# Windowed attention stage of a two-layer decoder: scores first in each unit, exponents ahead of the projections' copies, shift ahead of the weights' copy

## What is computed

```
q, k, v = x @ Wq.T, x @ Wk.T, x @ Wv.T        # 16 query heads, 4 key heads, head size 128
q, k = rms_norm(q), rms_norm(k)               # over the head, times (1 + w)
q = q * cos + rotate_half(q) * sin            # k likewise
scores = q . k / sqrt(128), masked to 0 <= distance <= 64
att = softmax(scores); ctx = att @ v
x = x + ctx @ Wo.T
```

## Time and profile before

| | us |
|---|---|
| median of three runs | 1591.7 (1590.38 to 1596.24) |
| the profiled execution, its own time | 1597.39 |
| its span, first to last instruction | 1595.6 |
| busy in the span: PE, DVE, ACT, POOL | 1339.1, 1099.5, 810.9, 629.7 |
| mean granted clock of PE | 0.929 of 2.4 GHz |
| the windowed stage, first normalised x to last output | about 729 to 1243 |

### The profile page before, as it was taken

One profiled execution on the slowest core, in us unless ns is written; L12 is line 12 of the kernel. 1 busy time (PEld: TensorE's weight loads), 2 busy tenths in 40 slices (PEclk: granted clock), 3 DMA queues, 4 the chain that ended last, 5 costly groups with the idle time before them and its releaser, 6 DMA issues. The chain is left out here.

```text
span 1595.6 us, 26439 instructions
## 1 busy us (share of the span) xinstructions
PE 1339.1 (84%) x7985; PEld 1027.9 (64%) x8032; DVE 1099.5 (69%) x2086; ACT 810.9 (51%) x1811; POOL 629.7 (39%) x693
## 2 busy tenths in 40 slices
PE   6775278888699999984898998998998788987998
PEld 3332155555588888873677776777776465656887
DVE  5999588889456767568777777777776466653443
ACT  2222078888454343435565665665665255652332
POOL 3220466556561000006666566656665333220000
PEclk9988589999799999996999999999999799998999
DMA  9000133331000000002000000000000000000000
GB/s 367 41 0 0 40 99 87 79 79 40 1 1 1 1 0 0 1 1 96 1 1 1 0 0 0 0 0 0 0 0 1 5 3 3 2 1 1 14 13 27
DMA packets 30303, 40.24 MB, mean 25 GB/s; under 512 B 4320, under 2 KB 25824, under 8 KB 28704
## 3 DMA queue, kind: packets, MB, share of 16 engines
q1 hardware_dynamic: 30240, 39.45, 7.9%
HBM read 28.96 MB, written 2.10 MB: 19 GB/s over the span
## 5 line engine op out<-in xcount | busy, mean ns | idle before, releaser
L1704 ACT ACTIVATE wi_weights<-wi_psum,wi_bias,wi_scale 128x128 f32<-128x128 f32 x256 | 113.9, 454 | 113.0 <-DVE wi_bias L1814 113.0
L1479 POOL TENSOR_TENSOR wi_straight<-wi_straight,wi_crossed 128x512 f32<-128x512 f32 x80 | 110.0, 1374 | 5.8 <-DVE wi_crossed L1800 5.7
L846 DVE TENSOR_REDUCE gq_top<-gq_psum 128x4 f32<-128x512 f32 x128 | 86.8, 678 | 32.0 <-PE gq_psum L733 31.2
L1467 POOL TENSOR_TENSOR wi_scratch<-wi_sums,wi_eps 128x4 f32<-128x4 f32 x80 | 35.9, 449 | 159.7 <-DVE wi_sums L1783 158.3
L1805 DVE TENSOR_REDUCE wi_top<-wi_psum 128x4 f32<-128x512 f32 x64 | 44.0, 688 | 74.7 <-PE wi_psum L1594 74.7
L800 ACT ACTIVATE gq_weights<-gq_weights 128x512 f32<-128x512 f32 x128 | 81.1, 634 | 25.2 <-DVE gq_weights L854 23.9
L1018 POOL TENSOR_TENSOR ex_scratch<-ex_squares,ex_eps 128x4 f32<-128x4 f32 x12 | 2.4, 201 | 231.0 <-ACT ex_junk L1129 231.0
L740 PE MATMUL gq_psum<-const,gq_weights 128*128 128x128 f32 x512 | 79.3, 278 | 14.9 <-ACT gq_weights_t L806 14.9
L1215 DVE TENSOR_TENSOR ex_gated<-ex_gated,ex_psum 128x512 f32<-128x512 f32 x64 | 43.9, 687 | 65.2 <-PE ex_psum L1070 53.9
L1142 ACT ACTIVATE ex_hidden_high<-ex_gated 128x512 fp32r<-128x512 f32 x64 | 40.4, 632 | 93.8 <-DVE ex_gated L1215 93.8
L854 DVE TENSOR_TENSOR gq_weights<-gq_psum,gq_top 128x512 f32<-128x512 f32 x128 | 87.2, 681 | 0.0
(11 more groups left out here) (339 smaller groups left out, 4086.0 us busy)
## 6 DMA issues: line engine op xcount, KB each, us to landing
gq_keys<-in_ctx_keys_dram SPq DMA_DIRECT2D x16, 512.0 KB, 3.8
gq_keys_diagonal<-gq_key_parts SPq DMA_DIRECT2D x64, 128.0 KB, 3.8
x<-in_x_dram SPq DMA_DIRECT2D x4, 512.0 KB, 9.3
gate<-in_gate_dram SPq DMA_DIRECT2D x2, 1024.0 KB, 5.5
up<-in_up_dram SPq DMA_DIRECT2D x2, 1024.0 KB, 7.5
down<-in_down_dram SPq DMA_DIRECT2D x2, 1024.0 KB, 9.3
wq<-in_wq_dram SPq DMA_DIRECT2D x1, 2048.0 KB, 19.6
wo<-in_wo_dram SPq DMA_DIRECT2D x1, 2048.0 KB, 25.5
```

Source lines behind the costliest of these rows:

```text
L846: dve.tensor_reduce(top[:, u % 4, :], rows(u), AX.X, ALU.max).then_inc(topped, 1)
L1479: added_up = pool.tensor_tensor(straight[:, at], straight[:, at], crossed[:, at], ALU.add)
L1704: act.activation(weights[:, g % 2, j, :], ps[:, SC + g % 2, j * P:j * P + P], ACT.Exp, bias=bias[:, g % 2, j:j + 1], scale=scale[:, g, j:j ...
```

## The change

Only orders change; no instruction is added or removed, and no tile or semaphore.
- PE: `scores` comes first in a unit, then all items' `project`, then `project_out`, `turn_weights`, `turn_heads`, `turn_h`, and `attend` last. At the end of the stage `project_out` of unit 2 precedes `turn_weights` of unit 3.
- ACT: `weigh` first, then `take` of the items, `take_turned`, and `take_attended` last.
- DVE: `shift` directly after `maximum`, then `take_weights`; in unit 0 `split_h` directly after that, ahead of `rotate`, where it was the unit's last.

Line numbers in the changed file are 5 lower on ACT and DVE behind the first edit. The diff:

```diff
--- before.py
+++ after.py
@@ -1620,22 +1620,15 @@
 
             def one(t, s, first, last):
                 for g in range(U):
-                    items = ahead(t, s, g, last)
-                    for item in items:
-                        if item[0] != "v":
-                            project(*item)
                     scores(t, s, g)
-                    for item in items:
-                        if item[0] == "v":
-                            project(*item)
-                    if g > 0 or not first:
-                        pt, _, pg = earlier(t, s, g, 1, U)
-                        turn_weights(pt, pg)
+                    for item in ahead(t, s, g, last):
+                        project(*item)
                     if g > 1 or not first:
                         pt, _, pg = earlier(t, s, g, 2, U)
                         project_out(pt, pg)
                     if g > 0 or not first:
-                        attend(*earlier(t, s, g, 1, U))
+                        pt, _, pg = earlier(t, s, g, 1, U)
+                        turn_weights(pt, pg)
                     if g < 3:
                         turn_heads("q", t, g + 1)
                     elif not last:
@@ -1643,6 +1636,8 @@
                         turn_heads("q", t + 1, 0)
                     if g == 0 and not last:
                         turn_h(t + 1, 1 - s)
+                    if g > 0 or not first:
+                        attend(*earlier(t, s, g, 1, U))
 
             turn_h(0, 0)
             for item in FIRST_ITEMS:
@@ -1651,8 +1646,8 @@
             turn_heads("k", 0, 0)
             turn_heads("q", 0, 0)
             pairs(pe, one)
+            project_out(NB - 1, 2)
             turn_weights(NB - 1, 3)
-            project_out(NB - 1, 2)
             attend(NB - 1, 1, 3)
             project_out(NB - 1, 3)
 
@@ -1713,12 +1708,9 @@
 
             def one(t, s, first, last):
                 for g in range(U):
+                    weigh(t, g)
                     for item in ahead(t, s, g, last):
                         take(*item)
-                    weigh(t, g)
-                    if g > 0 or not first:
-                        pt, _, pg = earlier(t, s, g, 1, U)
-                        take_attended(pt, pg)
                     if g < 3:
                         take_turned("q", t, s, g + 1)
                     elif not last:
@@ -1726,6 +1718,9 @@
                         take_turned("q", t + 1, 1 - s, 0)
                     if g == 0 and not last:
                         take_turned("h", t + 1, 1 - s)
+                    if g > 0 or not first:
+                        pt, _, pg = earlier(t, s, g, 1, U)
+                        take_attended(pt, pg)
 
             act.wait_ge(net.in_attn1, 16 * 4)
             for name in PIECES[:2]:
@@ -1837,11 +1832,13 @@
                     if g == 0 and not last:
                         normalise(t + 1, 1 - s)
                     maximum(t, g)
+                    shift(t, g)
                     if g > 0 or not first:
                         pt, _, pg = earlier(t, s, g, 1, U)
                         take_weights(pt, pg)
-                    shift(t, g)
                     items = [item for item in ahead(t, s, g, last) if item[0] != "v"]
+                    if g == 0 and not last:
+                        split_h(t + 1, 1 - s)
                     for item in items[:1]:
                         rotate(*item)
                     invert(t, g)
@@ -1852,8 +1849,6 @@
                     if g > 0 or not first:
                         pt, _, pg = earlier(t, s, g, 1, U)
                         split_out(pt, pg)
-                    if g == 0 and not last:
-                        split_h(t + 1, 1 - s)
                 own.again()
 
             aggregate(dve, net, aggregated)
```

## The result

| | before | the change |
|---|---|---|
| median, us (4 runs each, same chip) | 1593.97 (1590.38 to 1597.19) | 1660.06 (1654.72 to 1660.58) |
| ratio, 95% interval | | 1.0398 (1.0378 to 1.0419) |
| profiled execution: own time, span | 1597.39, 1595.6 | 1654.72, 1652.9 |
| one step in the loop | 30.64 | 34.81 |
| PE busy, and its mean granted clock, 830 to 1130 us | 271.95, 0.94 | 247.20, 0.97 |

The change is 66 us slower; 1645 was forecast, and 1660 lies in the range. The step is worked out from `finish`, which runs once in each: eleven steps lie between its starts at 828.8 and 1211.7. 15 steps x 4.17 is 63 of the 66 us. The two profiled executions bear that out: from the first normalised x to the last output the stage takes 513.8 us before and 576.1 in the change, 62.3 more.

A forecast was written before the change was run, and what follows sets the result against it. Bound before: PE in units 0 to 2, one DVE chain in unit 3. Four legs sum to 34.1 us a step against 30.64; 15 x 3.5 = 53 us more gives a median of 1645, range 1620 to 1672.

The forecast's parts named there:

- one ring: On DVE and ACT: shift, exponents, raw, square, rotate, inverse, `split_out`, maximum follow each other back to shift; plain 6.52 us.
- The signs named in advance: DVE idle ahead of sums, its scores wait nearly gone, ACT waiting for shift, PE's longest wait `split_out` in all units.
- unit 0 to 1: 7.76 us: the plain 6.52 and 1.24 for `split_h`, with its input h_high, ahead of `rotate`.
- unit 1 to 2: 7.42 us, with 0.90 added for `finish` between inverse and `split_out`.
- unit 2 to 3: 11.2 us: 4.65 from inverse to `split_out`, q0's rotation running beside POOL, and 0.2 for late `take_weights`.
- unit 3 to 0: 7.7 us: next x's `normalise` (0.54) ahead of the maximum, and 0.7 for PE's weighted sum at slow clock.
- the shift "at nothing": DVE's shift starting while POOL works was taken to cost 0, the tile being 4 columns wide.
- rival C: POOL holds up DVE's shift: 1.7 us a step on top, 35.8, time 1670; 20 in 100.
- Costs nothing by itself: PE does the same matmuls in another order, free by itself; the question is when each wait is met.
- Saves its 0.6 on this ring: DVE's shift moved ahead of `take_weights` saves 0.6, already in the 0.71 from maximum to shift.
- Rival A: Faster: DVE has slack, PE runs without its unit-3 stall, gaining 4.5 us a step, 1524; 5 in 100.
- Rival B: No change: POOL's normalise and join fall elsewhere, 2.5 us of contention goes, 30.7 a step, 1592; 8 in 100.

The follow-up runs named there:

- experiment 2: Kernel before, with only ACT's order swapped: exponents ahead of the items' raw and square; 1687.72 us, 1.0594.
- experiment 12: Kernel before, with DVE's shift ahead of `take_weights` and ACT's exponents ahead of raw and square; 1661.57 us, 1.0422.
- experiment 4: The change, with the shift done as four one-column operations, the scale as each one's scalar; 1658.75 us, 1.0409.
- experiment 1: The change, with ACT's raw and square of the items put back ahead of the exponents; 1626.67 us, 1.0208.
- experiment 8: The change, with ACT's raw and square back ahead of the exponents and PE's `turn_weights` back ahead of `project_out`; 1590.78 us, 0.9985.
- experiment 7: Kernel before, with only DVE's shift moved ahead of `take_weights`; 1572.6 us, 0.9871.
- experiment 5: Kernel before, with both of unit 2's rotations ahead of the inverse on DVE; 1564.08 us, 0.9812.
- experiment 6: The change, with both of unit 2's rotations ahead of the inverse on DVE; 1635.11 us, 1.0259.
- experiment 9: Kernel before, with the shift ahead of `take_weights` and both of unit 2's rotations ahead of the inverse; 1564.41 us, 0.9821.
- experiment 10: Kernel before, with shift ahead of `take_weights`, unit 2's rotations ahead of the inverse, and `project_out` ahead of `turn_weights` in unit 3 alone; 1568.76 us, 0.9841.

## Why the prediction was right, and where it was not

**The direction and the mechanism were right.** What was two chains side by side became one ring over DVE and ACT: experiment 2 makes the loss with that swap alone, and experiment 12 makes the change's step, 34.94 against 34.81. The signs named in advance came: DVE idle ahead of sums and ahead of `split_h`, DVE's wait for scores gone, ACT waiting for the shift, PE's stall for `split_out` in unit 3. That PE's longest wait would be for `split_out` in all units did not come; elsewhere it waits for the turned q.

**The four legs**, between the starts of the shifts, in the round shown (over the steps of the loop the first swings between 7.96 and 8.18, the third between 10.82 and 10.92, and the means sum to 34.81):

| leg | forecast | measured | what the difference is |
|---|---|---|---|
| unit 0 to 1 | 7.76 | 7.96 | shift 0.43, 0.27 more than alone |
| unit 1 to 2 | 7.42 | 7.40 | |
| unit 2 to 3 | 11.2 | 10.92 | shift 0.48 more; inverse to `split_out` 3.84, not 4.65 |
| unit 3 to 0 | 7.7 | 8.46 | shift 0.76 more, x's normalise 0.98, not 0.54; the 0.7 for slow PE work did not come |
| sum | 34.1 | 34.7 | |

- **The step that failed is the shift "at nothing".** It was taken at 0 "since the tile is 4 columns wide". The rows have 0.27, 0.48 and 0.76 over the 0.16 that it takes alone, 1.5 a step, near the 1.7 that rival C gave it. That the sums agree is partly luck: C had 0.2, 0.5 and 1.0 for the shifts that end legs 0 to 1, 1 to 2 and 3 to 0, which measure 0.02, 0.48 and 0.27, and nothing for the one that ends leg 2 to 3, the longest wait of all, 0.76. The rule of the Trainium skill ("SBUF — State Buffer", section "Who interferes with whom") that the prediction quoted and set aside, exclusion for a whole instruction however small, agrees with these rows: each long shift ends within 0.02 of POOL's operation. Experiment 4 ties the wait to the instruction that reads two tensors. Of C, then, the mechanism came and not the sum.
- **Two terms were too high and hid that.** Leg 2 took the collision over whole, 4.65 from inverse to `split_out`, since neither engine's order changes there. The orders do not, but which of the two starts first does: DVE's cosine product now comes 0.03 ahead of POOL's `normalise` and not 0.25 behind it, takes 0.68 and not 1.34, and the stretch is 3.84. Leg 3 had 0.7 for a weighted sum at the slow clock. The clock did fall, to 0.50 from 1052 to 1055, and held `split_out` up by 0.1 at most: `take_attended` ends at 1058.50 and `split_out` starts at 1058.53, 0.18 behind the inverse, where it is 0.09 in unit 0. Between 870 and 1200 that leg is 8.46 to 8.48 in steps with a slow stretch and in steps without. Take 0.8 and 0.7 off 34.1, add 1.5 for the shift and 0.4 for the normalise, and 34.5 is left, against 34.74 from the rows. Terms 1.5 too high and 1.9 too low nearly cancel: that the sum came within 0.7 of the step is in part luck.
- **"Costs nothing by itself" was wrong for PE's order.** Transposes behind `project_out` give `take_weights` late: in the round shown it starts 2.90 after the shift in unit 2 and 3.14 in unit 3, where the forecast let it start by 2.5. PE then waits for it. The loss was hidden under the ring, and shows once that is undone: experiment 1 stays at 32.25, and experiment 8, with PE's order back too, comes to 30.15. In the change both chains bind nearly together: in unit 2 `take_weights` ends at 1045.06 and the square at 1045.25. The 0.2 allowed for this in leg 2 was the one place where the forecast looked, and it looked at DVE alone.
- **"Saves its 0.6 on this ring" undervalued the shift's move.** Made alone it is worth 21 us (experiment 7), by less idle time of PE, most of it from the same turn of the collision, and, in the profiled execution, a clock that stays up. The other parts of the change together then cost 88 us on a base of 1572.6, and not 66 on 1594.
- **Rival A** needed the square without the exponents, and no row has that. **Rival B** needed the collision to go; from the first step on, the pair takes 2.66 to 2.69 once a step in every kernel here in which the inverse stands ahead of q0's rotation, and in none in which it stands behind (experiments 5, 6, 9 and 10).
- **From step to total**, 15 x 4.17 is 63, where 15 x 3.5 was 53. The rest of the miss of 15 us is 2.3 for the median of before (1594.0, not 1591.7) and 3.5 that the steps do not hold.

Left open: the price of the long shifts by itself (experiment 4 traded a wait for as long an operation), and what holds experiment 8 at 1591, 18 us above experiment 7, whose orders are otherwise alike up to scores first, `attend` and `take_attended` last and `split_h` early. In experiment 8 POOL's `normalise` is first again, by 0.13 to 0.32, and from the inverse to `split_out` are 4.59 to 4.67 us, some 0.75 more than in experiment 7; what of the 18 us that makes was not tested.

## What to carry to other kernels

Where engines run strictly in order, write down for a reordered piece whether its input now stands behind its own consumer's output on another engine, and add up that ring through all its instructions; a swap that leaves every instruction as it is can cost 6% (experiment 2). After the binding ring look for the next one below it, since a fix of the first alone gives back only the distance between them (experiments 1 and 8). Where two engines collide, a stretch measured in one kernel can't be carried over whole to another: 0.3 us in the start of one of them decided here which of the two paid. And a later release can be the cure: moving the inverse behind the second rotation made the kernel 1.9% faster, more than any other single edit here.

## What the runs showed of the hardware

- A DVE operation on 128x4 with two tensor inputs in SBUF waits for POOL as a large one does: 0.16 us alone, 1.25 beside L1479 in experiment 6, median 0.53 over the change. The same product as four one-column operations with the scale as scalar took 0.20 to 0.22 each, 256 times out of 256.
- x's normalise, which reads one tile and two columns as scalars, took 0.40 at least and 1.11 in the median in the change, against 0.54 before; it now starts under POOL's L1489 in most steps.
- Where q0's cosine product on DVE and POOL's `normalise` overlap, the one that starts second takes longer: DVE 1.34 and POOL 1.04 where POOL starts 0.25 ahead (before), DVE 0.68 and POOL 1.54 where DVE starts 0.03 ahead (the change and experiment 7), in every step of the loop. In the three collisions before that lie outside the loop POOL starts 0.14 ahead, and DVE takes 1.45.
- PE's granted clock was 0.50 behind 14 of 14 stalls of 2.67 to 2.70 us in the kernel before, with 9 of 14 of 2.14 to 2.25 in the change, and 1.00 behind all of 1.68 to 1.73 in the profiled execution of experiment 7. There a step is 1.59 us shorter for 0.95 us less of that idle. The length of the stall alone does not settle it: one of 2.65 before, at 780.1, and one of 2.73 in the change, at 773.5, had no such stretch behind them.
